# A four-stage transformer block on one core: the second attention regrouped into four 32-row groups, and the stages of a step placed anew

## What is computed

```
x = x + attn_a(layernorm(x));  x = x + ffn(layernorm(x))
x = x + attn_b(layernorm(x));  x = x + ffn(layernorm(x))
```

## Time and profile before

| | us |
|---|---|
| median of three runs | 3087.94 (3087.81 to 3092.41) |
| the profiled execution | 3091.3 |
| its span, first to last instruction | 3089.5 |

### The profile page before, as it was taken

The page is one execution under the profiler, slowest core; times in us unless marked ns, Lnnn a source line. Parts: engine busy times, 40 slices in busy tenths (PEclk is TensorE's granted clock), DMA queues, the critical chain, the costliest instruction groups (busy, mean ns, idle before and its releaser), DMA issues. The chain is left out here.

```text
span 3089.5 us, 73872 instructions
## 1 busy us (share of the span) xinstructions
PE 2913.1 (94%) x24644; PEld 2292.2 (74%) x24644; DVE 2358.1 (76%) x5980; ACT 1844.8 (60%) x3717; POOL 461.3 (15%) x1047
## 2 busy tenths in 40 slices
PE   5799999999999999999999999999999999999987
PEld 4677777777777777777777777777777777777765
DVE  5577788777788777788777788777788777788754
ACT  2366665566665566665566665566665566665555
POOL 4111111111111111111111111111111011111010
PEclk8899999999999999999999999999999999999998
DMA  2000000000000000000000000000000000000000
GB/s 65 8 11 17 16 16 3 14 16 16 16 16 3 14 16 16 16 16 3 14 16 16 16 16 3 14 16 16 16 16 3 14 16 16 16 16 3 15 10 17
DMA packets 42114, 44.83 MB, mean 15 GB/s; under 512 B 2640, under 2 KB 41424, under 8 KB 42064
## 3 DMA queue, kind: packets, MB, share of 16 engines
q1 hardware_dynamic: 42064, 44.20, 4.7%
HBM read 21.12 MB, written 16.78 MB: 12 GB/s over the span
## 5 line engine op out<-in xcount | busy, mean ns | idle before, releaser
L983 ACT ACTIVATE f_r<-HID,b1c 128x512 f32<-128x512 f32 x512 | 352.6, 689 | 525.0 <-PE HID L430 523.0
L450 PE MATMUL Y<-w2t,f_hh 128*128 128x256 f32 x2048 | 550.5, 301 | 5.3 <-DVE f_hl L1324 5.3
L450 PE MATMUL Y<-w2t,f_hl 128*128 128x256 f32 x2048 | 513.0, 283 | 0.0
L1324 DVE TENSOR_TENSOR f_hl<-f_r,f_hh 128x512 fp32r<-128x512 f32 x512 | 351.9, 687 | 130.3 <-ACT f_hh L984 122.2
L430 PE MATMUL HID<-ff_xh,w1t 128*128 128x512 f32 x1024 | 435.5, 425 | 4.6 <-DVE ff_xl L1316 4.6
L450 PEld LDWEIGHTS Y<-w2t,f_hh 128*128 128x128 f32 x2048 | 389.8, 190 | 49.1 <-issue 28.9
L430 PE MATMUL HID<-ff_xl,w1t 128*128 128x512 f32 x1024 | 407.0, 397 | 0.0
L450 PEld LDWEIGHTS Y<-w2t,f_hl 128*128 128x128 f32 x2048 | 391.7, 191 | 3.2
L984 ACT ACTIVATE f_hh<-HID,b1c 128x512 fp32r<-128x512 f32 x512 | 350.9, 685 | 0.0
L1161 ACT ACTIVATE a_qz<-Q 128x512 f32<-128x512 f32 x512 | 280.1, 610 | 2.8 <-PE Q L782 2.7
L1430 DVE TENSOR_TENSOR a_s<-Q,cst 128x512 f32<-128x512 f32 x384 | 248.8, 682 | 42.1 <-PE Q L576 42.1
(11 more groups left out here) (192 smaller groups left out, 7248.4 us busy)
## 6 DMA issues: line engine op xcount, KB each, us to landing
x<-in_x SPq DMA_DIRECT2D x32, 512.0 KB, 4.2
out<-x SPq DMA_DIRECT2D x32, 512.0 KB, 3.1
b_vm<-b_v SPq DMA_DIRECT2D x64, 96.0 KB, 2.1
x<-in_w SPq DMA_DIRECT2D x2, 512.0 KB, 4.5
a_s<-in_w_qkv SPq DMA_DIRECT2D x1, 768.0 KB, 5.1
ff_xn<-in_w SPq DMA_DIRECT2D x1, 512.0 KB, 6.6
f_r<-in_w SPq DMA_DIRECT2D x1, 512.0 KB, 7.0
cst<-in_const SPq DMA_DIRECT2D x1, 389.0 KB, 5.6
```

The costliest lines, as they stand in the source:

```text
L450: mm = pe.matmul(Y[t // 2][:, (t % 2) * D:(t % 2 + 1) * D], h[:, fb % 2, t * P:(t + 1) * P], w2t[:, fb, :], start=False, stop=(fb == FB - ...
L983: act.activation(f_r[:, fb % 2, :], banks[fb % 2][:], ACT.Relu, bias=b1c[:, fb:fb + 1]).then_inc(f_rr, 1)
L1324: dve.tensor_tensor(f_hl[:, fb % 2, :], f_r[:, fb % 2, :], f_hh[:, fb % 2, :], ALU.subtract).then_inc(f_lo, 1)
```

## The change

- **Second attention, layout.** A head's query is stacked once as high and low (32 rows) and its key twice over: pass m = 0 is the high part on both halves, m = 1 the low part on both. Two key passes then sum the same four terms. The four key heads are four groups of 32 rows that work side by side, each with a bank of its own (Q[3], Q[0], Q[1], HID[1]). The stacked queries now take four transposes for a tile, the keys still two; stack_hi and stack_lo handle half as many query columns.
- **A tile's scores in one visit.** scores(t) writes the masks of both query blocks (from tables with one 32-row half for each pass, line 777's successor) and then all 16 score products; exps(t) makes four passes of 512 columns; numer(t) takes both blocks. Four visits for a sequence instead of eight.
- **One FFN bank.** HID[1] now holds scores, so in phase 2 too every up(fb) uses HID[0] and waits for relu(fb - 1). The layer norm in front of an FFN in phase 2 is transposed in two halves through HID[0] (f_half), the second after DVE has read the first.
- **Turned queries** of tiles 1 to 3 and all turned keys but the first go through Q[2], which they share with turn_numer, turn_y and project: turn_q(t) waits for residual(t - 2), turn_k(t) for the evacuation of turn_q(t).
- **Stages placed anew** on every engine, in both phases. On POOL the FFN's rstd moves ahead of sines(1).
- The constant table grows from 778 to 1290 columns, and DVE makes three casts from it instead of one.

```diff
-        A_SCORES = (Q[3], Q[0], Q[1], HID[1])
+        A_SCORES = B_SCORES = (Q[3], Q[0], Q[1], HID[1])
...
-            if t < 2:
-                return (Q[2], Q[3], Q[2])[j]
-            return HID[(t, t + 1, t)[j] % 2]
+            return Q[3] if j and t == 0 else Q[2]
...
+            def f_half(turn, hf):
+                if turn is None:
+                    return
+                if hf:
+                    pe.wait_ge(ff.lo, turn * 2 + 1)
+                elif needed(turn * FB):
+                    pe.wait_ge(f_act, turn * FB)
+                norm_half(ff, turn, hf, HID[0])
...
-                        f_up(own if fb < UPS else carry, fb, turn_a)
+                        f_up(own if fb < UPS else carry, fb, turn_a, ONE_HID)
...
+                    def turn_q(t):
+                        pe.wait_ge(b_lo, b * NT + t + 1)
...
+                        elif t == 1:
+                            pe.wait_ge(b_te, b * 8 + 1)
+                        else:
+                            pe.wait_ge(b_out, b * NT + t - 1)
+                        for r in range(REP):
+                            mm = pe.transpose(turn_bank(t, 0)[:, r * P:(r + 1) * P].bitcast(F32R),
+                                              b_qs[:, t % 2, KVH * r:KVH * (r + 1)].rearrange("p h s d -> p (h s d)"), ident_r[:])
...
+                    def mask(bl, g, m, blocks=1):
+                        n, at_col = blocks * REP, bl % 2 * REP * W
+                        table = qodd_rows if bl else qfirst_rows
+                        pe.matmul(B_SCORES[g][:, at_col:at_col + n * W].rearrange("p (u q) -> p u q", u=n),
+                                  table[rows_of(g), m, :], hot[rows_of(g), m, :].unsqueeze(1).broadcast_to([BR, n, W]),
+                                  start=(m == 0 and (guarded or bl % 2 == 0)), stop=False, skip_group_check=True)
...
+                    def scores(t):
+                        pe.wait_ge(b_te, b * 8 + 2 * t + 2)
...
+                            pe.wait_ge(b_ne, b * NT + t)
+                            pe.wait_ge(b_ex, (b * NT + t) * KVH)
...
+                        for m in range(2):
                             if t:
+                                for g in range(KVH):
+                                    mask(2 * t, g, m, 2)
                             else:
+                                for bl in range(2):
+                                    for g in range(KVH):
+                                        mask(bl, g, m)
+                        for bl in (2 * t, 2 * t + 1):
+                            for m in range(2):
+                                for g in range(KVH):
+                                    mm = score(bl, g, m)
+                                    if bl % 2 and m:
+                                        mm.then_inc(b_s[g], 1)
```

More of the change, by code:

```diff
@@ L727, in next_norm @@
                     def next_norm(half):
[L728 to L739, removed]
+                        at_half(turn_a, half, own, carry)
@@ L747, in turn_qk @@
[L747 to L754, removed]
@@ L775, in mask @@
[L775 to L779, removed]
-                    def score(bl, g2, gp):
-                        return pe.matmul(Q[g2][:, gp * REP * W:(gp + 1) * REP * W], keys(bl, g2, gp, P),
-                                         b_qT[64 * g2:64 * g2 + 64, gp, bl, :],
-                                         start=False, stop=not guarded, skip_group_check=True)
@@ L878, in phase2 @@
                     up(5)
+                    up(6)
                     down(4)
-                    up(6)
+                    turn_q(0)
+                    turn_k(0)
+                    scores(0)
+                    down(5)
                     up(7)
-                    turn_qk(0, 0)
-                    turn_qk(0, 1)
-                    down(5)
-                    turn_qk(0, 2)
-                    scores(0)
-                    down(6)
-                    scores(1)
-                    own_norm()
@@ L922, in phase2 @@
[L922 to L937 removed]
+                    numer(0)
@@ new lines, in phase2 @@
+                    turn_q(1)
+                    down(6)
+                    own_norm(0)
+                    turn_k(1)
+                    down(7)
+                    turn_numer(0)
+                    own_norm(1)
+                    scores(1)
+                    turn_y(0)
+                    up(0)
+                    project(0)
+                    numer(1)
+                    turn_q(2)
+                    up(1)
+                    turn_k(2)
+                    down(0)
+                    turn_numer(1)
@@ new lines, in phase2 @@
+                    scores(2)
+                    turn_y(1)
+                    up(2)
+                    project(1)
+                    turn_q(3)
+                    numer(2)
+                    next_norm(0)
+                    turn_k(3)
+                    down(1)
+                    scores(3)
+                    next_norm(1)
+                    turn_numer(2)
+                    down(2)
+                    turn_y(2)
+                    numer(3)
+                    qk(s.next_a, 0, b)
@@ L938, in phase2 @@
+                    project(2)
+                    up(3)
+                    turn_numer(3)
+                    qk(s.next_a, 1, b)
+                    turn_y(3)
+                    up(4)
+                    down(3)
                     project(3)
@@ L1096, in phase1 @@
                     values(1)
+                    keys(0)
                     own_norm()
@@ new lines, in phase2 @@
+                    evacuate_q(1)
+                    own_norm(0)
+                    evacuate_k(1)
+                    own_norm(1)
+                    stack_hi(2)
+                    y_hi(0)
+                    exps(1)
+                    relu(0)
+                    evacuate_q(2)
+                    evacuate_numer(1)
+                    stack_hi(3)
+                    evacuate_k(2)
+                    relu(1)
+                    y_hi(1)
+                    exps(2)
+                    relu(2)
```

506 lines of the change are left out of this document (218 added, 288 removed).

## The result

The changed kernel takes 3047.15 us (median of 4 runs, 3042.93 to 3048.64); the kernel before, run beside it, 3089.26. The ratio is 0.986, interval 0.9843 to 0.9877: faster by 42 us. The forecast was 3074, 14 us faster: right in direction, a third of the size. Ratios leave out slow executions; the only one in all runs took 9125.48 us, in the experiment with one tile split, where it lifts the median of five to 3060.86 from the 3058.6 of the other four.

What follows compares the result with a forecast made beforehand. TensorE, busy for 94% of the span, was taken as the bound. Terms of -2.0 + 3.5 - 2.0 = -0.5 us a step over some 31 steps, with the start -14 in all, gave 3074 us; range 3008 to 3130.

Steps and rivals of the forecast that it cites:

- Work, -2.0: TensorE's work: fewer transposes, score visits, narrow-block exits and numerator visits, less 0.1 for split norm transposes; -2.0 us a step.
- the upper bound of 1.5 and its rival: Phase 2 score visits last up to 1.5 us if four groups run short of abreast; +1.7 a step, 3127, chance 0.08.
- Waits of phase 2, +3.5: TensorE's waits in phase 2 grow from 1.9 to 5.4 us a step; bounds 1.9 to 6.5 after.
- (a): Start of phase 2: up(6) waits until the bank it shares with up(5) is free; 1.76 us.
- (b): First turned queries of phase 2 wait on the chain from phase 1's last residual; 0.4 us left beside the bank wait.
- (c): First scores of phase 2 wait for the evacuation behind turn_k(0); 0.96 us, where it was 0.48.
- (d): numer(0) of phase 2 waits for four exps, partly covered by down(5) and up(7); 0.3 us.
- (e): up(0) of phase 2 waits for the second half of its norm on DVE; 0.9 us.
- (f): turn_q(3), right behind project(1) on the same bank, waits for its residual in phase 2; 0.65 us.
- The folding rival: Waits of phase 2 fold together, so half of +3.5 does not appear; -2.25 us a step, 3020, chance 0.22.
- Waits of phase 1, -2.0: More work ahead of each consumer cuts phase 1's waits from 2.7 to 0.7 us a step; bounds 0 and -2.7.
- The clock rival: About 3.1 us of waiting in some 8 of phase 2 halves the clock; 1.7 to 2 a step, 3128, chance 0.17.

Runs made afterwards that it cites:

- the experiment with one tile split: The changed kernel with the numerators of phase 1's second tile in two visits again, the first tile's projection between them: 3060.86 us, ratio 0.9894.
- the edit that uncovers the masked scores: The changed kernel with down(7) and state(1) ahead of phase 1's first scores again, on TensorE alone: 3093.45 us, ratio 1.0017.
- One swap of two blocks: The changed kernel with down(4) between up(5) and up(6) at the start of phase 2, instead of behind up(6): 3080.33 us, ratio 0.9977.
- the shorter chain with the swap: The changed kernel with less work ahead of the first turned queries on three engines, and down(4) between up(5) and up(6): 3056.56 us, ratio 0.9904.
- the qkv products behind: The changed kernel with all four qkv products behind the last projection of phase 1, instead of two inside the last tile's chain: 3120.96 us, ratio 1.012.
- three steps of the last: The changed kernel with shorter chain, tile 0's numerators merged, down(6) ahead of turn_q(1), and up(5) ahead of the last qkv product: 3029.71 us, ratio 0.9821.

## Why the prediction was right in direction and wrong in size

*Work, -2.0: right for phase 2.* TensorE's busy time there fell by 1.92. A score visit takes 1.01 to 1.02 where the row of the first attention gave 1.08, so four groups do run abreast with half-length products; the upper bound of 1.5 and its rival fall. The Trainium skill (TensorE: Matmul & The Clock Gate, Measured speedup vs the span model) gives 3.07 for four row groups, by which the forecast had an estimated 1.1 for the columns alone; the trace, with both ends in 1.01, does not agree for this shape.

*Waits of phase 2, +3.5: right.* Idle time there grew by 3.43. Single terms, block to block: (a) 1.61 (1517.34 to 1520.81 less two blocks of 0.93) for 1.76; (b) 0.55 (down(4) 1.50 instead of 0.95) for 0.4; (c) 0.94 (1522.32 to 1523.81 less the 0.55 of six transposes) for 0.96; (d) 0.30 (up(7) 1.23 instead of 0.93) for 0.3; (e) 0.95 (1533.42 to 1534.57 less 0.20) for 0.9; (f) 0.78 (project(1) 1.58 instead of 0.80) for 0.65. The folding rival fell.

*Waits of phase 1, -2.0: this is the term that failed.* Phase 1 lost 3.22, and the same lists under the old attention took it from 50.80 to 47.53, while the old lists under the new attention took 50.90. So the size belongs to the order of phase 1. The mistake was to count that phase in waits alone. In phase 2 I had priced two numerator blocks in one visit and the product behind a narrow block; the same reorder in phase 1, two more pairs side by side, I read only as a way to cover masks. By the split of one pair, 0.33 to 0.35 each, that is some 0.7 a step of work which I had put at nothing. The remaining 2.5 or so I take for waits, near the far end of my bounds (0 to -2.7): the list of TensorE's waits in phase 1 is empty after the change, where I had left 0.7, its idle time is 0.21, and the five places with a wait before add up to 2.4. Of these the masked scores gave 1.3 and the norm's transposes 0.7. Which move in the lists removed which wait was not separated by a run: the edit that uncovers the masked scores brought another wait with it.

*The sum.* -0.5 forecast, -1.68 measured a step (92.75 to 91.07, medians of the middle steps), times 30 is -50 us instead of -15; the start and the end took about what was set aside for them. The missing 1.2 a step is the term above. (The rival of phase 1 comes by its own sum to 3133, not 3130.)

*The clock rival* did not occur in the changed kernel, though 2.5 us of idle time do stand in 6.5 there, near what I had named as its condition. The condition was incomplete: the sum of the waits does not decide it alone. One swap of two blocks with the same sum set it off in nearly every middle step, and two more kernels (the old attention with the new phase 1, the shorter chain with the swap) show it in most of theirs. Its price, 1.7 to 2 in the forecast, was 1.7 a step under the old attention and less in the others: 1.1 after the swap, 1.3 with the qkv products behind, mostly 0.7 with the shorter chain and the swap.

## What to carry to other kernels

When a change reorders a stage, price the work of the new order there as well as its waits: how often the array is entered and left by narrow blocks is part of an order. Read the phases apart: the regrouping that gives this change its name made its own phase 1.5 us longer, and the reorder beside it took twice that out of the other. Before moving a wait, look at what stands between it and the next one; after the swap above, two waits that only transposes separate cost more than their length. And an order taken over on one engine alone, as with state(1) here, prices the mismatch and not the order; an edit that uncovers a wait which both kernels cover prices the cover and not the change.

## What the runs showed of the hardware

The granted clock fell in middle steps of four of these kernels, and in three steps of the last, though no single wait close ahead of it was longer than some 1.8 us: in one kernel 1.73 with eight transposes behind it, in the others two shorter ones with transposes between them. The changed kernel has such a pair too, of 0.40 and 0.79, and its clock stayed at 1.00 in every middle step, so how much idle time it takes there is not shown. With equal idle time and equal work in the 6.47 us ahead it fell in one order and not in the other: 0.55 over the next 3.80 us against 1.00 over the next 3.79. One rival had four row groups lose something on products half as long as those of the first attention; a visit of them took 1.01 to 1.02 instead, against 1.08 there, so nothing was lost to the shorter products.
